# One two-layer kernel: the first mixer begins in another order, its weight halves are made in pieces

## The reference, cut to what matters

```python
xn = _layernorm(x)
y = xp[:, 0:Tv] * w_dw[:, 0] + xp[:, 1:Tv + 1] * w_dw[:, 1] + xp[:, 2:Tv + 2] * w_dw[:, 2]
y = jnp.einsum('btd,ed->bte', y, w_pw)
x = x + y
qkv = jnp.einsum('btd,ed->bte', x, w_qkv)...
q, k = _apply_rope(q, sin, cos), _apply_rope(k, sin, cos)
q_phi, k_phi = jax.nn.elu(q) + 1.0, jax.nn.elu(k) + 1.0
kv = k_phi[..., :, None] * v[..., None, :]
kv_prefix, k_prefix = jnp.cumsum(kv, axis=1), jnp.cumsum(k_phi, axis=1)
attn = einsum(q_phi, kv_prefix) / (sum(q_phi * k_prefix) + 1e-06)
x = x + sigmoid(delta @ w_gate + b_gate) * (attn @ w_o)
...
hid = jax.nn.silu(jnp.einsum('btd,efd->btef', h, w1) + b1)      # 4 dense experts
h = jax.nn.gelu(jnp.einsum('ncd,ndh->nch', xe, W1) + b1)        # 16 routed experts
```

## Time and profile before

| | |
|---|---|
| median of 3 runs | 1199.7 us (1199.05 to 1200.12) |
| the profiled execution's own time | 1197.8 us |
| its span, first to last instruction | 1196.1 us |
| the same span on PE | busy 1138.2 us, 95% |
| the mixer (beats), on the trace's clock | about 20 to 147 us |
| experts of the first layer | about 147 to 335 us |
| second layer | from about 336 us on |

### The profile page before, as it was taken

The page is one execution under the profiler, slowest core; times in us unless marked ns, Lnnn a source line. Parts: engine busy times, 40 slices in busy tenths (PEclk is TensorE's granted clock), DMA queues, the critical chain, the costliest instruction groups (busy, mean ns, idle before and its releaser), DMA issues.

```text
span 1196.1 us, 31475 instructions
## 1 busy us (share of the span) xinstructions
PE 1138.2 (95%) x11940; PEld 751.9 (63%) x11948; DVE 819.7 (69%) x2041; ACT 688.4 (58%) x1376; POOL 832.8 (70%) x1111
## 2 busy tenths in 40 slices
PE   4999999999979999999999999999999999999997
PEld 1344566678736666667666766666676666676665
DVE  4778878613776876786687578668668767866552
ACT  3543363357335666576566656666666665765665
POOL 0787432102444987978888798788879879788895
PEclk9999999999999999999999999999999999999998
DMA  8300010113034220302302031040212203023001
GB/s 309 138 1 1 1 45 19 48 51 93 23 70 87 70 46 14 83 6 46 79 21 46 20 81 32 16 90 11 46 44 57 46 17 80 6 46 81 2 3 37
DMA packets 74891, 60.19 MB, mean 50 GB/s; under 512 B 38962, under 2 KB 69298, under 8 KB 73652
## 3 DMA queue, kind: packets, MB, share of 16 engines
q1 hardware_dynamic: 73716, 56.08, 18.8%
q0 software_dynamic: 1024, 2.09, 0.6%
HBM read 19.76 MB, written 4.72 MB: 20 GB/s over the span
## 4 chain that ended last, share of the span: by engine, by line
PE 68%; ACT 2%; DVE 1%; issue 1%; DVEq 0%
PE S L1980 10%; PE S L1981 10%; PE S L1982 10%; PE A L1970 9%; PE O L1994 6%; PE O L1995 5%; PE O L1992 5%; PE M L1961 3%; PE M L1938 2%; PE M L1940 2%; PE M L1939 2%; PE M L1955 1%; PE M L1948 1%; PE M L1946 1%; PE M L1947 1%
## 5 line engine op out<-in xcount | busy, mean ns | idle before, releaser
L1722 POOL TENSOR_TENSOR plow<-prob 128x512 f16<-128x512 f32 (+3 forms) x640 | 588.5, 931 | 94.5 <-ACT prob L2198 70.4
L2198 ACT ACTIVATE prob<-S,keep_sigma 128x512 f32<-128x512 f32 (+3 forms) x640 | 396.1, 626 | 263.7 <-PE S L1982 260.8
L2299 DVE CUSTOM_DVE_ANT_0 junk<-A,mask_rows,part 128x512 bf16<-128x512 f32 (+3 forms) x384 | 248.9, 648 | 98.0 <-PE A L1970 76.8
L1992 PE MATMUL O<-V,prob 128*128 128x65 f16 x2176 | 232.7, 193 | 0.2 <-POOL plow L1722 0.2
L1994 PE MATMUL O<-V,prob 128*128 128x64 f16 x2176 | 232.5, 194 | 0.0
L1995 PE MATMUL O<-V,plow 128*128 128x65 f16 x2176 | 231.7, 192 | 0.0
L1980 PE MATMUL S<-rows 97*128 97x512 f16 (+3 forms) x640 | 223.1, 349 | 3.8 <-ACT prob L2198 3.5
L1981 PE MATMUL S<-rows 96*128 96x512 f16 (+3 forms) x640 | 222.3, 347 | 0.0
L1970 PE MATMUL A<-rows 96*128 96x512 f16 (+3 forms) x640 | 221.0, 346 | 1.3 <-DVE part L2299 1.0
L1982 PE MATMUL S<-rows 96*128 96x512 f16 (+3 forms) x640 | 220.7, 345 | 0.0
L1992 PEld LDWEIGHTS O<-V,prob 128*128 128x128 bf16 x2176 | 203.0, 97 | 23.6 <-POOL plow L1722 0.3
(11 more groups left out here) (388 smaller groups left out, 1845.3 us busy)
## 6 DMA issues: line engine op xcount, KB each, us to landing
rows<-stage_rows SPq DMA_DIRECT2D x64, 256.0 KB, 3.4
V<-stage_v SPq DMA_DIRECT2D x16, 516.0 KB, 4.6
W<-in_W SPq DMA_DIRECT2D x2, 2048.0 KB, 14.2
shifted<-turned SPq DMA_DIRECT2D x32, 128.0 KB, 2.2
rows<-stage_pos SPq DMA_DIRECT2D x64, 64.0 KB, 3.1
w<-in_w SPq DMA_DIRECT2D x2, 1024.0 KB, 10.6
xe_rows<-zero SPq DMA_DIRECT2D x1, 1280.0 KB, 5.3
ye_rows<-xe SPq DMA_DIRECT2D x5, 256.0 KB, 3.2
```

What stands on the lines that cost most here:

```text
L1722: pool.tensor_tensor(plow[:, k % PB, 0:w], full, full.bitcast(BF16).rearrange("p (q e) -> p q e", e=2)[:, :, 1], ALU.subtract).then_inc(s_ ...
L1992: pe.matmul(both, high[:, cs, 1], vh[h][:, j, 0:HS + 1], start=(j == 0 and s == 0), stop=False, skip_group_check=True)
L2198: act.activation(prob[:, k % PB, 0:w], S[k % 2][:, 0:w], ACT.Exp, scale=sigma[:, 2 * p + h:2 * p + h + 1]).then_inc(s_exp, 1)
L2299: dve.tensor_tensor_reduce(junk[:, g % 2, 0:w], A[g % 2][:, 0:w], add, -1.0, before, ALU.add, ALU.min, out).then_inc(s_max, 1)
```

## The change

It has three parts.

The start of the mixer is ordered anew. Only two of the four turns come ahead of the first `Y`; the third and fourth turn follow in beats -9 and -8. DVE normalises eight of its tiles in two halves with the three taps between them, ACT takes its tiles and evictions by turns. The semaphore of the first weights, seven loads before, is cut in three: `s_w` for the two that the taps need, `s_table` for cosine, sine and gate bias, `s_rows` for the value weights and the selector.

The halves of `w1` leave the start. The load goes behind five others and counts into `s_later`. The maximum is taken in four pieces of 512 columns in beats 4 to 7 and put together in beat 8, the sum over partitions comes in beat 13, the scales in beat 15; ACT's eight pieces come in beats 17 to 24, DVE's four in beats 20, 22, 24 and 26; POOL's three small products move from beat -4 to 16.

In `experts0` a Gelu on one column is put ahead of ACT's copies of the turned tokens.

```diff
-        order = [("T", c) for c in range(NC)]
-        for c in range(-1, NC + 1):
+        order = [("T", 0), ("T", 1), ("Y", 0), ("T", 2), ("K", 0), ("KS", 0), ("T", 3), ("Q", 0), ("QS", 0), ("G", 0)]
+        for c in range(0, NC + 1):
...
-            for dst, src in ((w_dw, "w_dw"), (w_sq, "w_sq"), (cos, "cos0"), (sin, "sin0"), (b_gate, "b_gate"),
-                             (w_vrep, "w_vrep"), (sel, "sel0")):
+            for dst, src in ((w_dw, "w_dw"), (w_sq, "w_sq")):
                 sp.dma_start(dst[:], dram[src]).then_inc(s_w, 16)
-
-            for name in FIRST_EXPERTS:
-                sp.dma_start(t0[name][:], dram[name]).then_inc(s_w1, 16)
+            for dst, src in ((cos, "cos0"), (sin, "sin0"), (b_gate, "b_gate")):
+                sp.dma_start(dst[:], dram[src]).then_inc(s_table, 16)
+            for dst, src in ((w_vrep, "w_vrep"), (sel, "sel0")):
+                sp.dma_start(dst[:], dram[src]).then_inc(s_rows, 16)
...
+            turned(0)
+            turned(1)
             pe.wait_ge(s_w, WLOAD)
...
+                if u in (-SC, 1 - SC):
+                    turned(u + SC + 2)
                 if going and m == 8:
                     finish(c - 1, m)
                 if u == UNITS - 4:
                     route_logits()
-                elif u == -SC:
+                elif u == 13:
                     bounds_summed()
...
+            normal(0)
+            normal(1)
+            turned(0)
+            normal(2)
+            turned(1)
+            normal(3)
...
-                elif u == 1 - SC:
-                    act.wait_ge(s_ln, 2)
-                    act.activation(w1_high, w1_all, ACT.Copy, scale=scales[:, 0:1])
-                    act.activation(w1_all, w1_all, ACT.Copy, scale=scales[:, 0:1]).then_inc(s_sqrt, 1)
+                elif 17 <= u < 17 + 2 * NC:
+                    at = span((u - 17) // 2)
+                    if u % 2 == 1:
+                        act.wait_ge(s_ln, 2)
+                        act.activation(w1_high[:, at], w1_all[:, at], ACT.Copy, scale=scales[:, 0:1])
+                    else:
+                        act.activation(w1_all[:, at], w1_all[:, at], ACT.Copy, scale=scales[:, 0:1]).then_inc(s_sqrt, 1)
...
-                if m == 5 and c == 0:
-                    dve.wait_ge(s_sqrt, 2)
-                    dve.tensor_tensor(w1_low, w1_all, w1_high, ALU.subtract)
...
-                if u == 1 - SC:
+                if 4 <= u < 4 + NC:
+                    dve.wait_ge(s_later, LATER_LOADS)
+                    dve.tensor_reduce(quarters[:, u - 4:u - 3], w1_all[:, span(u - 4)], AX_X, ALU.max,
+                                      apply_absolute_value=True).then_inc(s_v, 1)
+                    steps[0] += 1
+                elif u == 4 + NC:
+                    dve.wait_ge(s_v, steps[0])
+                    bound_parts()
+                elif u == 15:
                     bound_scales()
+                elif 20 <= u < 20 + 2 * NC and u % 2 == 0:
+                    c = (u - 20) // 2
+                    dve.wait_ge(s_sqrt, 2 + c)
+                    dve.tensor_tensor(w1_low[:, span(c)], w1_all[:, span(c)], w1_high[:, span(c)], ALU.subtract)
+                    c = u // SC
...
             def routed():
                 act.wait_ge(s_hl, 2 * NC)
+                act.activation(gmax[:, 0:1], scales[:, 0:1], ACT.Gelu_apprx_tanh)
                 for c in range(XC):
```

More of the change, by code:

```diff
@@ L167, in layernorm @@
     step(dve.tensor_tensor(rstd[:], rstd[:], newt[:], ALU.mult))
-FIRST_EXPERTS = ("w1", "ln_g", "ln_b")
-LATER = ("wg", "rank_order", "w_mg", "b1", "w2", "b2", "below", "W1", "W2", "be1", "be2")
+LATER = ("w1", "ln_g", "ln_b", "wg", "rank_order", "w_mg", "b1", "w2", "b2", "below", "W1", "W2", "be1", "be2")
 def mixer0(nc, dram, keep, t0):
@@ L220, in mixer0 @@
         s_x, s_w, s_v = [sem(f"x_loaded{c}") for c in range(NC)], sem("w0_loaded"), sem("dve_step0")
-        s_later, s_w1 = sem("later_loaded"), sem("w1_loaded")
+        s_table = sem("tables0_loaded")
+        s_later, s_rows = sem("later_loaded"), sem("row_weights_loaded")
         s_ln, s_sqrt, s_norm = sem("ln_var0"), sem("ln_sqrt0"), sem("ln_ready0")
         s_xn, s_xna = sem("xn_tiles0"), sem("xn_tiles0_act")
-        s_pad, s_unit, s_taps = sem("pads0"), sem("unit_set"), sem("taps_made")
+        s_pad, s_taps = sem("pads0"), sem("taps_made")
         s_g, s_gf = sem("general_sums0"), [sem(f"general_out{i}") for i in range(2)]
@@ L314, in _ @@
             sp.wait_ge(s_later, LATER_LOADS)
-        WLOAD = 16 * 7
+        WLOAD, TABLES, ROW_WEIGHTS = 16 * 2, 16 * 3, 16 * 2
         @block.tensor
@@ L418, in bounds_summed, with turned @@
                 pe.wait_ge(s_rd, 1)
+                pe.wait_ge(s_rec, 1)
                 pe.matmul(BOUND, keep["ones"][:], parts[:, 0:2], start=True, stop=True).then_inc(s_rl, 1)
-            for c in range(NC):
+            def turned(c):
                 begin(("T", c))
@@ L435, in beat @@
                 if value(u + 3) is not None:
+                    if u == -3:
+                        pe.wait_ge(s_rows, ROW_WEIGHTS)
                     rows(value(u + 3))
@@ L469, in projections @@
                 elif m == 6:
+                    if c == 0:
+                        act.wait_ge(s_table, TABLES)
                     wait_sum(act, ("G", c))
@@ L501, in _, with normal, turned @@
             act.wait_ge(s_norm, 1)
[L502 to L505, removed]
+            def normal(c):
+                for i in range(TPC * c + 1, TPC * (c + 1), 2):
+                    act.activation(xn_tok[:, i, :], x_tok[:, i, :], ACT.Identity, bias=nmr[:, i:i + 1],
+                                   scale=rstd[:, i:i + 1]).then_inc(s_xna, 1)
+            def turned(c):
                 wait_sum(act, ("T", c))
                 out(("T", c), act.activation(xnT[:, span(c, 2)], bank(("T", c))[:], ACT.Copy))
-            act.wait_ge(s_w, WLOAD)
+            normal(0)
[4 more added lines that the diff above has]
+            normal(3)
             def beat(u, c, m, coming, going):
@@ L576, in beat @@
                     projections(c + 1, m)
-                if u == 5 - SC:
+                if u == 16:
                     pool.wait_ge(s_ln, 2)
@@ L671, in bound_scales @@
                 dve.reciprocal(scales[:, 0:2], tops[:, 0:2]).then_inc(s_ln, 1)
-            dve.memset(U[:, 0:1], 1.0).then_inc(s_unit, 1)
+            step(dve.memset(U[:, 0:1], 1.0))
             dve.memset(last[:], 0.0).then_inc(s_last, 1)
@@ L690, in _, with normal @@
             dve.scalar_tensor_tensor(nmr[:], mv[:, :, 0], -1.0, rstd[:], ALU.mult, ALU.mult).then_inc(s_norm, 1)
-            for i in range(0, NT, 2):
-                dve.tensor_scalar(xn_tok[:, i, :], x_tok[:, i, :], mv[:, i, 0:1], rstd[:, i:i + 1], ALU.subtract,
-                                  ALU.mult).then_inc(s_xn, 1)
+            def normal(a, b):
+                for i in range(a, b, 2):
+                    dve.tensor_scalar(xn_tok[:, i, :], x_tok[:, i, :], mv[:, i, 0:1], rstd[:, i:i + 1], ALU.subtract,
+                                      ALU.mult).then_inc(s_xn, 1)
+            normal(0, 2 * TPC)
             dve.wait_ge(s_w, WLOAD)
@@ L698, in _ @@
             dve.tensor_scalar(taps[0], w_sq[:, 0, :], w_dw[:, 0:1], None, ALU.mult).then_inc(s_taps, 1)
-            dve.wait_ge(s_unit, 1)
-            bound_parts()
+            normal(2 * TPC, NT)
+            dve.wait_ge(s_table, TABLES)
             def bc(t, n):
@@ L749, in early_tiles @@
                 first = slice(0, EARLY)
-                dve.wait_ge(s_sqrt, 3)
+                dve.wait_ge(s_sqrt, 2 + NC)
                 step(dve.reciprocal(rstd[:, first], std[:, first]))
```

7 lines of the change are left out of this document (3 added, 4 removed).

## The result

The changed kernel takes 1192.05 us (median of 4 runs, 1191.22 to 1192.50) against 1199.91 us for the kernel before on the same chip (1199.05 to 1201.55). The ratio is 0.9939, with a 95% interval of 0.9927 to 0.9951, which is 5.9 to 8.8 us. On another chip, later, it was 0.9956 (0.9941 to 0.9972). The profiled pair differs by less than the medians: spans of 1190.3 and 1196.1 us, 5.8 us.

The account below looks back on a forecast made before the run. PE, busy 95% of the span, was taken as the bound, with time won only where it waits or works slowly. 4.0 + 2.0 + 2.1 - 0.3 - 1.9 + 1.3 = 7.2 us off 1199.7 gave 1192.5 us, range 1190.0 to 1196.6.

Parts of the forecast that it names:

- (a): Start of the mixer: `Y` begins sooner, at about 15.7 instead of 19.66; 4.0 us gained.
- rival 3: First `Y`: TensorE reaches its higher clock within it, capped by the loads; 0.8 us more gained, 1191.7; chance 0.07.
- (b): From `Y` to the first prefix sum: shorter waits at `K` and POOL's sum; 2.0 us gained, prefix sum at about 34.5.
- (c): Chunk 0, first prefix sum to chunk 2's `Y`: 21.3 us instead of 23.4; 2.1 gained, bounds 0 and 3.9.
- (d): Chunk 1: small sum on PE and two scale steps on DVE ahead of the gated product; 0.3 us lost.
- (e): Chunk 2: three DVE subtractions ahead of the gated product lose 1.4 us, ACT's eighth piece 0.5.
- (f): Start of the experts: Gelu's table load moves into ACT's idle time; 1.28 us gained, bounds 0 and 1.59.
- The loads: Beat 4: DVE arrives at 43.1, last load at about 42.8, no wait; further start gain beyond 0.3 us is eaten.
- rival 1: Chunk 0: DVE's added work becomes the next bound, small-step ordering costs 0.5 more; 4.6 us gained, 1195.1; chance 0.17.
- rival 2: Dense beats: DVE's subtractions contend with POOL for ports; 1.9 us lost or more, say 1194.9; chance 0.13.
- Rivals 4 and 5: Late loads stop beat 4, slower from about 50.5 (0.06); late-freed `general` bank costs at most 1.4 us, 1193.9 (0.05).

Follow-up runs that it names:

- order-alone run: Changed order of turns, products and loads, with the Gelu column, but `w1`'s maximum, copies and subtraction whole at the start, against the kernel before: ratio 1.0011.
- kernel with no reduction in chunk 0: Changed kernel with all `w1` work moved into DVE's waits (reductions at beat 17, subtractions at 34): 1187.97 us, ratio 0.9911 to the kernel before.
- subtractions at 26: Changed kernel with DVE's four subtractions together at beat 26 and ACT's last piece a beat earlier: 1192.12 us, ratio 0.9955 to the kernel before.
- own semaphore: Changed kernel with loads of `w1`, `ln_g`, `ln_b` counted by a separate semaphore: ratio 0.9938 to the kernel before; again on another chip, 1192.20 us, 0.9946.

## Why the prediction was right, and where its steps were wrong

1192.5 us were forecast and 1192.05 measured; the range held it. But the total is better than its steps. By the profiled pair:

| step | forecast | measured | by which rows |
|---|---|---|---|
| zero sooner (not the change, see below) | 0 | +0.5 | 13.10, 12.55 |
| (a) `Y` begins | +4.0 | +4.0 | 19.66, 15.15, less the 0.5 |
| `Y` to its eviction (rival 3) | 0 | +1.4 | 5.57, 4.19 |
| (b) first eviction to prefix sum | +2.0 | +2.3 | 15.33, 13.03 |
| (c) to `Y` of chunk 2 | +2.1 | -1.5 | 23.41, 24.94 |
| (d) `Y` of chunk 2 to chunk 1's gated product | -0.3 | -0.2 | 63.97 to 82.26, 57.31 to 75.83 |
| (e) chunk 2 | -1.9 | -2.8 | 60.76, 63.75, less (d) |
| (f) Gelu's table | +1.3 | +1.4 | 1.59, 0.23 |
| sum | 7.2 | 5.1 | |

In the trace the first Gelu's row moved by 5.36 us and the end by 5.8. The medians moved by 7.9 us on that chip and 6.3 on the next, so the forecast's 7.2 lies inside the spread, and part of the agreement is luck.

**(a), (b), (f)** were right in mechanism, and in this pair in size. `Y` starts 2.60 us behind `nmr` in every run that has the new order, to 0.01 us. In the old order it starts when `sel` has landed: 6.56, 7.86 and 8.94 us behind `nmr` in the three profiles, with DVE waiting 3.37, 4.66 and 5.75 us, so the 4.0 us are the smallest of three values, by luck the one that the forecast was read from. The 0.5 us of the zero are spread as well: the run with the Gelu alone, whose start is the old one, has its zero at 12.48. In (b), the rest of the chain behind POOL's first sum took 9.46 us again (22.91 to 32.37), as forecast. The order-alone run shows that (a) gives nothing while the bounds of `w1` stand ahead of `K`. On (f), where the Trainium skill (ScalarE: Activation LUTs, What ACT_TABLE_LOAD costs) has a drain of 1380 ns beside the load of 1283 ns, the rows show 1.28 us of load, the next instruction 1.29 us behind its start, and 1.36 us gained: no drain, as the prediction took it.

**Rival 3 came true**, though I gave it 0.07: `Y` took 1.4 us less, where the rival, capped by the loads, had 0.8. That this is TensorE's level is read from the length of the products alone (of `Y`'s six rows, two take 2.05 us in both kernels, four 3.62 and 2.32); the granted clock is listed as 1.00 from 14 to 26 us in both traces. Nor is the size the change's own: with the new order `Y` took 3.76 to 4.95 us in seven profiles, with the old one 5.06 to 5.57 in three. Of what followed, the prediction said that the loads would eat any further gain. They ate more.

**(c) is the step that failed.** Two parts of it have to be kept apart. The first is the sentence under "The loads" that DVE reaches beat 4 at 43.1 and "just does not wait". With rival 3's surplus DVE was there at 40.9 and waited 1.38 us. The cap I had named would have cost that wait; it cost 2.8 us (24.94 against 22.15 in the runs in which it is absent), since PE's wait grew by 1.2 us (3.02 against 1.80) and its next four products ran near the lower level (2.05 and 1.69 us against 1.10 and 1.02, 1.6 us). That these belong together is seen in three runs without a load wait and two with it; that the clock fell because of the longer wait is argued from their order in time, not shown by a kernel that changes only it. The second is the added work on DVE. The forecast of 21.3 us was met by the kernel with no reduction in chunk 0 (21.42), and the reductions added 0.7 (22.15): rival 1 in small. A part of this is rival 2's mechanism in chunk 0: behind the reductions, DVE's `phi` met POOL's `z` and took 1.57 us in the three runs without a load wait (46.43, 1.51 us, in the rows shown), 0.73 in the kernel without reductions there. My sum had fitted 3.4 us of work into 3.9 us of waits, without asking whether the work stands at the beats at which DVE waits. The sizes were right: the reductions took 0.65 to 0.69 us.

**(e)** was right in kind and too small by 0.9; it is the term whose size failed most after (c). The three subtractions cost 2.2 us instead of 1.4, because two of them took 1.34 and 1.23 us in place of 0.6, beside POOL, whose products there took 1.72 and 1.45 us instead of 1.27; the third took 0.66, and then POOL's `z` beside it 1.63. This is rival 2's mechanism, at 0.8 us where it named 1.9 and more. By the Trainium skill (GPSIMD Engine Reference, Specifications) POOL contends with DVE instructions of two SBUF inputs; the trace agrees, in that a reduction, with one, took 0.66 us beside POOL's `z` at 45.26, and POOL's two `z` 2.50. ACT's piece cost 0.57, forecast 0.5.

**Rivals 4 and 5** have no row that speaks for them, unless the load wait above counts as the beginning of 4: its point of decision was far away (50.5 in the prediction; by its own numbers, 43.1 and 7.2, it is 50.3).

Removing a wait of 2.9 us, or 1.7 us of contention, left the time as it was. In all four such profiles the last stretch of the table is 1.3 to 1.6 us longer, with products at the lower level in it or, with the subtractions at 26, shortly ahead of it. That is half to all of what had been gained; the rest is within the spread of the runs. Why the clock falls there stays open. Except with the subtractions at 26, the slow products begin right behind the 32 small products of `route_logits` (128x16, 3.64 us), but the same products stand in the kernel before and in the changed one's first profile with no fall behind them. The run with the Gelu alone has such a stretch too (7.49 us; granted clock 0.70 from 130 to 135 us), though it removed no wait in the mixer. And each kernel but the changed one and the own semaphore has one profile.

## What to carry to other kernels

Work that is put into an engine's spare time must stand at the beats at which that engine waits, not only fit into the sum of its waits: the same pieces of `w1` cost 3.0 us of chunks 1 and 2 along the beats and 0.5 inside the waits. A reordering of the start and the removal of work from it can be worth nothing apart (here one gave nothing, the other, with the Gelu column, 1.5 per mille, on one chip) and 4 to 6 per mille together, on two others, so test a gain of several edits as a whole as well as in parts. When one place is sped up, look at which load is only just in time there.

## What was not expected of the hardware

- An operation on one column can take as long as a large one beside it: DVE's 128x1 step took 1.08 us (53.54 to 54.62), and ended with POOL's 128x512 product beside it (53.35 to 54.61). In the repeat of the own semaphore it took 0.45, and the next such step 1.30. POOL's 128x1 product took 1.29 us beside DVE's subtractions.
- The stretch at TensorE's lower level moved between two executions of the same kernel, from 50 to 55 us (granted clock 0.70) to 120 to 130 us (0.88 and 0.77), with little change in the sum.
- The kernel before takes 1224.29 us on one chip and 1199.91 and 1198.89 on two others, and the ratios of the two variants that were run on two chips still agree within 0.2%: 0.9939 and 0.9956 for the changed kernel, 0.9938 and 0.9946 for the own semaphore.
